# Softmax exponentials per head on ScalarE, with the negated maximum as bias and the row sums from the accumulator; the stencil's order and the loads' pacing changed with it

## What is computed

```python
def layer0(x):                      # x: normalised
    q, k, v = 1x1 convolutions of x, cut into 8x8 windows, 6 heads of 32
    o = irfft2(rfft2(q * scale) * rfft2(k))         # per window, per channel
    attn = softmax(o @ v.T + bias)                  # 64 x 64 per window and head
    return proj(attn @ v)
def layer1(x):                      # x: normalised
    return merge_1x1(x + laplacian3x3(x)) + b
x = x + layer0(gn(x))
x = x + layer1(gn(x))
```

## Time and profile before

| | |
|---|---|
| median of 3 runs | 6189.45 us (6188.16 to 6193.84) |
| the profiled execution | 6202.11 us, span 6200.3 us |
| PE (matmuls) | 5885.3 us busy, 95% |
| VectorE | 5323.9 us, 86% |
| ScalarE | 3168.6 us, 51% |
| GpSimd | 2028.7 us, 33% |
| mean granted TensorE clock | 0.99 of full speed |
| HBM traffic | 87 GB/s over the span |

### The profile page before, as it was taken

One profiled execution on the slowest core, in us unless ns is written; L12 is line 12 of the kernel. 1 busy time (PEld: TensorE's weight loads), 2 busy tenths in 40 slices (PEclk: granted clock), 3 DMA queues, 4 the chain that ended last, 5 costly groups with the idle time before them and its releaser, 6 DMA issues.

```text
span 6200.3 us, 209925 instructions
## 1 busy us (share of the span) xinstructions
PE 5885.3 (95%) x93708; PEld 5173.1 (83%) x93708; DVE 5323.9 (86%) x8287; ACT 3168.6 (51%) x6020; POOL 2028.7 (33%) x1286
## 2 busy tenths in 40 slices
PE   7999999999999999999999999999999999999987
PEld 5888888888888888888888888888888888888876
DVE  4777788998998989898899889999889998888876
ACT  3555555554555555555555555555455555555531
POOL 1333333333333333333333333333333333333320
PEclk9999999999999999999999999999999999999999
DMA  4221133333334233332333323433333332322335
GB/s 127 70 68 45 56 90 97 92 86 88 92 93 106 68 87 108 94 85 79 102 92 98 94 75 87 114 92 82 82 99 92 99 86 68 81 77 68 90 87 157
DMA packets 392597, 550.78 MB, mean 89 GB/s; under 512 B 24918, under 2 KB 284825, under 8 KB 391706
## 3 DMA queue, kind: packets, MB, share of 16 engines
q1 hardware_dynamic: 391708, 537.35, 32.4%
HBM read 335.93 MB, written 201.33 MB: 87 GB/s over the span
## 4 chain that ended last, share of the span: by engine, by line
PE 80%; ACT 9%; DVE 8%; issue 3%; DMA 1%; SPq 0%; DVEq 0%
PE b_q L477 22%; PE b_t L566 10%; PE b_s L583 7%; PE b_q L552 7%; PE b_t L542 6%; PE b_s L485 5%; PE b_s L482 5%; PE b_s L428 3%; PE b_t L524 3%; PE b_s L430 3%; PE b_t L514 2%; ACT qkh L932 2%; ACT probs L996 2%; DVE qkl L867 2%; PE b_s L437 2%
## 5 line engine op out<-in xcount | busy, mean ns | idle before, releaser
L1039 POOL TENSOR_TENSOR probs<-probs,srec 128x768 f32<-128x768 f32 x512 | 900.2, 1758 | 2039.3 <-DVE srec L915 2039.3
L1028 POOL TENSOR_TENSOR probs<-probs,smax 128x768 f32<-128x768 f32 x512 | 754.5, 1474 | 1814.1 <-DVE smax L878 1814.1
L932 ACT ACTIVATE vs<-b_q 128x192 f32<-128x192 f32 x1024 | 339.5, 332 | 1399.4 <-PE b_q L477 1399.4
L873 DVE TENSOR_TENSOR probs<-b_s,posb 128x768 f32<-128x768 f32 x512 | 487.2, 952 | 477.5 <-PE b_s L583 476.0
L477 PE MATMUL b_q<-wnh,xh 128*128 128x288 f32 x2048 | 706.2, 345 | 67.4 <-DVE qkl L867 66.1
L867 DVE TENSOR_TENSOR qkl<-b_q,qkh 128x384 fp32r<-128x384 f32 x1024 | 566.4, 553 | 217.0 <-ACT qkh L932 182.5
L485 PEld LDWEIGHTS b_s<-yT,wp 128*128 128x128 f32 x4096 | 619.5, 191 | 55.8 <-issue 2.4
L485 PE MATMUL b_s<-yT,wp 128*128 128x128 f32 x4096 | 623.1, 275 | 1.6 <-issue 1.6
L482 PE MATMUL b_s<-yT,wp 128*128 128x256 f32 x2048 | 616.1, 383 | 4.0 <-DVE probs L873 2.2
L477 PE MATMUL b_q<-wnl,xhl 128*128 128x288 f32 x2048 | 610.9, 298 | 2.1 <-issue 2.1
L477 PE MATMUL b_q<-wnh,xl 128*128 128x288 f32 x2048 | 609.3, 297 | 2.5 <-issue 2.5
(11 more groups left out here) (155 smaller groups left out, 13948.4 us busy)
## 6 DMA issues: line engine op xcount, KB each, us to landing
ld<-in_x SPq DMA_DIRECT2D x192, 512.0 KB, 4.8
late<-x_dram SPq DMA_DIRECT2D x112, 640.0 KB, 6.9
xs<-in_x SPq DMA_DIRECT2D x128, 512.0 KB, 5.8
x_dram<-late SPq DMA_DIRECT2D x128, 512.0 KB, 3.1
out<-late SPq DMA_DIRECT2D x128, 512.0 KB, 5.8
late<-x_dram SPq DMA_DIRECT2D x240, 192.0 KB, 7.3
xs<-in_x SPq DMA_DIRECT2D x128, 256.0 KB, 6.6
x_dram<-late SPq DMA_DIRECT2D x128, 256.0 KB, 3.7
```

The costliest lines, as they stand in the source:

```text
L932: return A.activation(o, i, ACT.Copy)
L1028: P.tensor_tensor(probs[:, i % 2, :, :], probs[:, i % 2, :, :], smax[:, i % 2, :].unsqueeze(2).broadcast_to([128, 12, N]), ALU.subtract).t ...
L1039: P.tensor_tensor(probs[:, i % 2, :, :], probs[:, i % 2, :, :], srec[:, i % 2, :].unsqueeze(2).broadcast_to([128, 12, N]), ALU.mult).then_ ...
```

## The change

In words:

- The maximum is written negated (`negmax`). GpSimd's subtraction goes. ScalarE computes exp(score + negmax) with the bias as an operand for each of the 12 rows apart, 64 columns each, and its accumulator gives the row's sum. The twelve are written in three groups of four (`exponentials`): before the split, in the place of the former exponential, and behind the copy of probsT.
- VectorE's row sum goes. The reciprocal waits for the last exponential.
- In the odd iterations `edges` (which is `neighbours` there) moves from behind the merge result to the place of the former row sum; the border stays where it was (`borders`).
- SyncE waits, within a block, for merge tasks of TensorE: the result store for iteration 1, the source load for iteration 3, the second statistics load for iteration 5.

The diff, without the renaming of semaphores:

```diff
--- before.py
+++ after.py
@@ -139,7 +139,7 @@
         vs, vT = sb("vs", [128, 8, C]), sb("vT", [128, 2, 2, 2, 128])
         osb, yT = sb("osb", [128, 6, N]), sb("yT", [128, 3, 2, N])
         qkh, qkl = sb("qkh", [128, 2, QK], F32R), sb("qkl", [128, 2, QK], F32R)
-        smax, ssum, srec = sb("smax", [128, 2, 12]), sb("ssum", [128, 2, 12]), sb("srec", [128, 2, 12])
+        negmax, ssum, srec = sb("negmax", [128, 2, 12]), sb("ssum", [128, 2, 12]), sb("srec", [128, 2, 12])
 
         xs = sb("xs", [128, 2, 3, WS * W])
         xh, xl, xhb, xhl = (sb(name, [128, 2, 512], F32R) for name in ("xh", "xl", "xhb", "xhl"))
@@ -334,13 +334,17 @@
             for blk in range(BLOCKS + 1):
                 v = blk - MERGE_LAG - 1
                 if 0 <= v < STRIPS:
+                    if blk < BLOCKS:
+                        sp.wait_ge(m_mm, m_count[8 * blk + 1])
                     result_store(v)
                 v = blk - STENCIL_LAG + 1
                 if 0 <= v < STRIPS:
+                    sp.wait_ge(m_mm, m_count[8 * blk + 3])
                     source_load(v)
                 img, c = divmod(blk + 1, NS)
                 if 2 * c < NL and img + 1 < B:
                     stat_load((img + 1) * NL + 2 * c)
+                    sp.wait_ge(m_mm, m_count[8 * blk + 5])
                     stat_load((img + 1) * NL + 2 * c + 1)
                 if 1 <= blk <= STRIPS:
                     x1_store(blk - 1)
@@ -810,6 +814,9 @@
                         neighbours(v, 2)
                     elif ph == 6:
                         stencil(v, 2)
+
+            def borders(it):
+                blk, ph = divmod(it, 8)
                 v = blk - STENCIL_LAG + 1
                 if ph == 7 and 0 <= v < STRIPS:
                     border(v)
@@ -875,7 +882,7 @@
                                     posb[:, :, :].unsqueeze(2).broadcast_to([128, 3, 4, N]), ALU.add
                                     ).then_inc(s_out, 1)
                     dve.wait_ge(s_out, n)
-                    V.tensor_reduce(smax[:, i % 2, :], scored(i), AX.X, ALU.max).then_inc(max_done, 1)
+                    V.tensor_reduce(negmax[:, i % 2, :], scored(i), AX.X, ALU.max, negate=True).then_inc(max_done, 1)
                 if pair(0):
                     remainders(2 * j)
                 if pair(1):
@@ -891,10 +898,7 @@
                 norms(2 * j)
                 if pair(0):
                     remainders(2 * j + 1)
-                if pair(2):
-                    i, n = pair(2)
-                    dve.wait_ge(exp_done, n)
-                    V.tensor_reduce(ssum[:, i % 2, :], scored(i), AX.X, ALU.add).then_inc(sum_done, 1)
+                edges(2 * j + 1)
                 if pair(4):
                     i, n = pair(4)
                     u, col = i // SD, (i % SD) * 32
@@ -911,7 +915,7 @@
                     last.then_inc(x1_done, 1)
                 if pair(2):
                     i, n = pair(2)
-                    dve.wait_ge(sum_done, n)
+                    dve.wait_ge(exp_done, n)
                     V.reciprocal(srec[:, i % 2, :], ssum[:, i % 2, :]).then_inc(rec_done, 1)
                 h = (j + 2) // 2
                 if j % 2 == 1 and 0 <= h < PAIRS // 4:
@@ -919,7 +923,7 @@
                     V.tensor_tensor(tokens(xhl, 1, h, CB), windows(1, h), tokens(xhl, 1, h).bitcast(F32), ALU.subtract
                                     ).then_inc(xhl_done, 1)
                 m_result(2 * j + 1)
-                edges(2 * j + 1)
+                borders(2 * j + 1)
                 norms(2 * j + 1)
                 statistics(2 * j + 1)
 
@@ -969,6 +973,15 @@
             def v_copy(i):
                 act.wait_ge(v_mm, i + 1)
                 copy(vs[:, i % 8, :], v_psum).then_inc(v_out, 1)
+
+            def exponentials(i, n, third):
+                act.wait_ge(max_done, n)
+                for s in range(4 * third, 4 * third + 4):
+                    row = probs[:, i % 2, s, :]
+                    last = A.activation(row, row, ACT.Exp, bias=negmax[:, i % 2, s:s + 1],
+                                        accum_out=ssum[:, i % 2, s:s + 1])
+                if third == 2:
+                    last.then_inc(exp_done, 1)
 
             def high(i):
                 act.wait_ge(qkv_mm, i + 1)
@@ -986,14 +999,13 @@
                 if pair(0):
                     v_copy(2 * j)
                     high(2 * j)
+                if pair(2):
+                    exponentials(*pair(2), 0)
                 split(h, 0 if j % 2 == 0 else 2)
                 if pair(0):
                     v_copy(2 * j + 1)
                 if pair(2):
-                    i, n = pair(2)
-                    act.wait_ge(sub_done, n)
-                    pr = probs[:, i % 2, :, :].rearrange("p s m -> p (s m)")
-                    A.activation(pr, pr, ACT.Exp).then_inc(exp_done, 1)
+                    exponentials(*pair(2), 1)
                 if pair(0):
                     high(2 * j + 1)
                     act.wait_ge(vT_mm, pair(0)[1])
@@ -1002,6 +1014,8 @@
                     act.wait_ge(pT_mm, pair(3)[1])
                     copy(probsT[:, :, :, :].rearrange("p i h n -> p i (h n)"), q_banks[:, 0:2, 0:6 * N]
                          ).then_inc(pT_out, 1)
+                if pair(2):
+                    exponentials(*pair(2), 2)
                 a_result(2 * j + 1)
                 if j % 2 == 0:
                     split(h, 1)
@@ -1022,12 +1036,6 @@
             P.memset(sm[:, :, :], 0.0)
             P.memset(ones[:, :], 1.0).then_inc(ones_done, 1)
             for j, pair in doubles():
-                if pair(2):
-                    i, n = pair(2)
-                    pool.wait_ge(max_done, n)
-                    P.tensor_tensor(probs[:, i % 2, :, :], probs[:, i % 2, :, :],
-                                    smax[:, i % 2, :].unsqueeze(2).broadcast_to([128, 12, N]),
-                                    ALU.subtract).then_inc(sub_done, 1)
                 h = (j + 2) // 2
                 if j % 2 == 1 and 0 <= h < PAIRS // 4:
                     pool.wait_ge(xh_done, 3 * h + 2)
```

More of the change, by code:

```diff
@@ L188, in program @@
             "v_mm", "qkv_mm", "t_mm", "vT_mm", "s_mm", "pT_mm", "y_mm", "proj_mm", "o_mm"))
-        lo_out, prod_done, s_out, max_done, sum_done, rec_done, x1_done = map(sem, (
-            "lo_out", "prod_done", "s_out", "max_done", "sum_done", "rec_done", "x1_done"))
+        lo_out, prod_done, s_out, max_done, rec_done, x1_done = map(sem, (
+            "lo_out", "prod_done", "s_out", "max_done", "rec_done", "x1_done"))
         v_out, hi_out, qh_out, vT_out, exp_done, pT_out, yT_out, o_out = map(sem, (
@@ L193, in program @@
         xh_done, xl_done, xhl_done = map(sem, ("xh_done", "xl_done", "xhl_done"))
-        sub_done, norm_done = map(sem, ("sub_done", "norm_done"))
+        norm_done = sem("norm_done")
         border_w, diag_done, nb_done, z_done = map(sem, ("border_w", "diag_done", "nb_done", "z_done"))
```

## The result

| | before | after |
|---|---|---|
| median of 13 runs each, us | 6195.32 (6177.33 to 6205.1) | 6172.84 (6166.72 to 6175.66) |
| ratio to before, with 95% interval | | 0.9965 (0.9956 to 0.9973) |
| span of the profiled execution, us | 6200.3 | 6172.3 |
| TensorE's stops of over 0.5 us that nothing explains | 59, 96.2 us | 7, 5.7 us |
| 74 doubles of the first blocks, us | 764 | 822 |

What follows compares the result with a forecast made beforehand. TensorE was busy 5885 of 6200 us, so only time between its doubles (passes of the loop over j) could change. ScalarE +124, VectorE -100 and stops -98 gave -74 from 6189, rounded to 6120 us; range 6015 to 6280.

Steps and rivals of the forecast that it cites:

- ScalarE, +124: Twelve exponentials at 0.32 us pitch make probsT 0.68 us late for TensorE in 183 doubles without merge pieces: +124 us.
- Rivals 1 and 2: ScalarE's accumulator: dear, TensorE waits at L542, 6371 us, chance 0.22 (1); costs nothing, 6017 us, chance 0.14 (2).
- The stops, -98: SyncE's waits shorten the block-end transfer burst, removing three quarters of 130 us of unexplained TensorE stops: -98 us.
- Rival 3: TensorE's stops don't come from the transfer burst, or move with its pieces: 6213 us; chance 0.11 together with rival 4.
- VectorE, -100: Without row sum and with neighbour sums moved, VectorE is no longer late to the scores: 100 us gained.
- item (b): VectorE comes late to the scores: 92 us in blocks' last doubles, about 48 in the first ones.
- Rival 4: VectorE's reciprocal waits for exponentials, scores late again, the 100 us lost: about 6215 us; chance 0.11 together with rival 3.
- The neighbours' move: VectorE's neighbour sums (L723), away from GpSimd's multiplication, fall from 1.52 to 0.69 us, freeing 0.83 us.
- The tail, 0: In the tail the source load, out 5 us later, costs +0 to +15 us, taken as 0.

Runs made afterwards that it cites:

- e1: Kernel before with only the three SyncE waits added; 6068.38 us, 0.9788 of before.
- e5: Kernel before with only the odd iterations' neighbour sums moved ahead of the row sum, border left behind; 6199.12 us, 1.0004 of before.
- e9: Kernel before, old softmax kept, with the three waits and both neighbour sums and border moved ahead of the row sum; 6041.78 us, 0.9745 of before.
- e14: Changed kernel with the border moved early and the reciprocal at the end of the pass, exponential groups kept; 6128.96 us, 0.9884 of before.
- e7: Kernel before with the softmax change alone, no neighbours' move and no waits; 6369.19 us, 1.0272 of before.
- e2: Changed kernel without the three SyncE waits; 6304.49 us, 1.0172 of before.
- e10: Changed kernel with exponentials in groups of 4, 2, 4 and 2, border early, reciprocal at the end of the pass; 6024.83 us, 0.9718 of before.
- e11: Kernel before with the first wait alone, holding the result store for the block's second merge task; 6062.46 us, 0.9778 of before.
- e12: Kernel before with the second wait alone, holding the source load for the fourth merge task; 6066.56 us, 0.9784 of before.
- e13: Kernel before with the third wait alone, ahead of the second statistics load; 6198.43 us, 0.9996 of before.
- e4: Changed kernel with the bias kept but no accumulator, row sums again a VectorE reduction ahead of the reciprocal; 6164.94 us, 0.9948 of before.

## Why the prediction missed its size

**ScalarE, +124: right.** The pitch is 0.33 us (0.32 forecast), the doubles of the first blocks take 10.8 or 11.0 (10.8 forecast), place 4 is 10.84 in the quiet block, and the wait is where it was put, at probsT. What TensorE pays: 822 - 764 = 58 in the first blocks and 109 x (11.06 - 10.42) = 70 in place 4, together 128. Rivals 1 and 2 fall with that pitch.

**The stops, -98: too small.** e1 takes 130 us alone by the medians and 138 in the traces, the waits in the changed kernel 128 to 132. Counted rightly (below), 44 of the stops lie in the second doubles and 9 in the first: 44 x (13.87 - 11.38) = 110 us and 9 x (13.26 - 11.47) = 16, together 126. The cautious "three quarters" was the wrong choice between 0 and 130; the upper end was the truth. Rival 3 falls. That only 34 of 54 stops lay in the second double was itself blurred by the miscount.

**VectorE, -100: the step that failed.** e1 against after, both with the waits and without the stops, prices all that VectorE's lighter list gave: place 1 +6 us over its blocks, place 2 -3, place 3 -19, together -15 where -100 was forecast. (Place 3 gets shorter by the neighbours' move alone too, 12 us in e5.) The term rests on item (b), "The last double of a block takes 10.94 on average, not 10.11 (92 us over 109)". This is a miscount. I took a new double wherever the score matmuls had a gap of more than 4 us, and one stop fell inside a group. The L583 rows of before, where it happens:

```profile
4438.33 0.93 PE L583 MATMUL b_s<-vT,osb 32*64 32x64 f32 x48
...
4449.41 0.92 PE L583 MATMUL b_s<-vT,osb 32*64 32x64 f32 x47
4453.48 0.36 PE L583 MATMUL b_s<-vT,osb 32*64 32x64 f32 x1 [3.15 <-issue]
...
4466.87 0.93 PE L583 MATMUL b_s<-vT,osb 32*64 32x64 f32 x48
```

The 47 and the 1 are one group. Counted as two, every later double got the name of its neighbour: for the last third of the full blocks the "last" doubles were third ones of about 12 us. Counted rightly, place 4 of before is 10.42 on average, 84 of 109 at 10.1, and 6 of the longer ones, at 13.6, come once in 64 doubles and stand in after too. So instead of 92 + 48 us of VectorE's lateness some 35 + 48 existed. None of the 35 shows as won, since place 4 grew. Of the 48 in place 1 none was won either, because their cause stayed: the border, which the prediction's list of what stands behind the reciprocal left out, runs beside GpSimd's multiplication in after as in before (1020 ns in both), and e9 and e14, which move it, bring place 1 down.

Between the profiled executions the terms are +127 (ScalarE), -138 (stops) and -15 (VectorE), which make the -27 of the table by the way they are formed. Of the forecast's -74 the ScalarE term was off by 3, the stops by 40 to the good, and VectorE by 85 to the bad: the second hid nearly half of the third. That the sign came out right owes something to this luck.

**Rival 4 came true as a wait, and its price is open.** "It needs a pitch above 0.4 too": at 0.33 the reciprocal waits in 493 doubles for 358 us already. With the neighbour sums behind that wait it is dear (e7). In after, where they stand ahead of it, VectorE is late in place 1, but no more often than in before, and the border is enough to account for that. e14 moves border and reciprocal together for 44 us, of which 29 are in place 1 of the trace; what the reciprocal's wait costs by itself no run shows.

**The neighbours' move** frees VectorE as costed (e5: 687 ns), but in before this time is worth nothing that the runs can tell; with the new softmax it pays for the reciprocal's wait (some 62 us, e2 against e7).

**The tail, 0: right.** From the start of the last scores to the end of the span are 225 us in before and 226 in after.

The change as made is thus a bad trade beside a good one: its waits alone give 0.9788, and the softmax takes back almost all of it. In e10, where no copy that TensorE needs stands behind more than four exponentials in a row and border and reciprocal are moved, it takes back nothing, and gains 17 us over e9.

## What to carry to other kernels

When an average over periods feeds a term, check that the periods keep their phase: compare the count of groups with the known number of iterations, and look at a histogram by place, not a mean; a group split by a stall shifts all names behind it. Before an engine's freed time is counted as gain, name the instruction that makes it late and check that the change touches it: here the border did that, and stayed. Before an operation on an in-order engine is made to wait for something new, add up everything behind it to the next deadline, and put it last if nothing needs it soon. A change with several parts is worth splitting before it is judged: here one part gave 130 us and another took 128.

## What was unexpected in the hardware

- TensorE stops for 0.5 to 3.3 us at a time, with nothing that the profile names, next to a long stretch of full DMA engines, and in the stop of the earlier trace rows it runs part of the time at its lower clock level right after. The idle time is 91 us, and with what goes along with it 130 of 6200. Either of two cuts of the burst, 8 or 18 us long, removes it (e11, e12); a wait ahead of the second statistics load does not (e13, 61 stops). How it comes about was not found.
- ScalarE's accumulator output is a second instruction of 193 ns in the records, which adds 0.09 us to the distance between starts (e4: 0.24 without, after: 0.33 with).
- The smallest VectorE instruction suffers most beside GpSimd's 128x768 multiplication: the border's 128x20 TENSOR_SCALAR takes 1340 ns there and 226 away from it (e9), a 128x512 sum of two tiles 1518 and 687. The stencil's 128x512 SCALAR_TENSOR_TENSOR takes 1006 in the mean of before, where 171 of 384 run beside GpSimd's subtraction for the split (L1034, 1412 ns), and 675 in after, where none does.
